# Joining VectorE's and GpSimd's weighted expert sums one step later in the first feed-forward

## What is computed

```
gates        = top-2 of softmax(x @ router_w + router_b), renormalised, zero elsewhere
expert_out_e = gelu(x @ expert_w[e] + expert_b[e])            e = 0..7
combined     = sum over e of gates[:, e] * expert_out_e
x            = layernorm(x + combined @ out_w + out_b)
```

## Time and profile before

| | us |
|---|---|
| median of 3 timed runs | 1030.12 (1030.11 to 1031.32) |
| the profiled execution's own time | 1035.02 |
| its span in the trace | 1033.2 |

### The profile page before, as it was taken

How to read it: one execution, slowest core, us unless ns; L and a number is a source line. 1 busy time by engine, 2 the same in 40 slices (tenths; PEclk the granted TensorE clock), 3 DMA queues, 4 the chain that set the end, 5 groups by cost and what they waited for, 6 DMA issues and landing times.

```text
span 1033.2 us, 23457 instructions
## 1 busy us (share of the span) xinstructions
PE 925.1 (90%) x8745; PEld 626.5 (61%) x8745; DVE 822.4 (80%) x2400; ACT 629.7 (61%) x1560; POOL 373.7 (36%) x605
## 2 busy tenths in 40 slices
PE   6888888887877988998899999999999999999996
PEld 4667676666663444433555566666666666667654
DVE  6999998989986687765799988888888888733566
ACT  6999998989862344343666655555555555432543
POOL 4333342530422545444233333333333333310085
PEclk8999999999986999999999999999999999999999
DMA  7202121100000000000266755555555655510001
GB/s 267 63 23 63 43 63 43 46 20 2 2 2 1 1 1 1 1 1 1 56 125 121 123 100 96 100 97 96 103 103 102 98 97 100 95 36 1 1 32 52
DMA packets 174626, 61.41 MB, mean 59 GB/s; under 512 B 169248, under 2 KB 170800, under 8 KB 174384
## 3 DMA queue, kind: packets, MB, share of 16 engines
q1 hardware_dynamic: 174512, 59.90, 28.7%
HBM read 15.83 MB, written 2.10 MB: 17 GB/s over the span
## 4 chain that ended last, share of the span: by engine, by line
PE 47%; DVE 31%; ACT 6%; POOL 5%; DMA 5%; issue 5%; SPq 0%; POOLq 0%; DVEq 0%; ACTq 0%
PE bank L353 11%; PE bank L355 11%; PE bank L354 11%; DVE s_sb L1135 7%; DMA pt_lo<-w_lo 5%; DVE pt_lo L1092 5%; DVE scr L1122 3%; DVE scr L1092 3%; PE bank L668 3%; PE bank L670 3%; PE bank L669 3%; DVE w_lo L1153 2%; ACT s_sb L850 2%; ACT scr L803 2%; POOL scr L1598 2%
## 5 line engine op out<-in xcount | busy, mean ns | idle before, releaser
L1135 DVE CUSTOM_DVE_ANT_0 s_sb<-bank,consts 128x512 f32<-128x512 f32 (+3 forms) x512 | 227.9, 481 | 23.3 <-PE bank L355 15.0
L852 ACT ACTIVATE s_sb<-s_sb,nm 128x512 f32<-128x512 f32 (+3 forms) x256 | 141.4, 553 | 103.8 <-DVE nm L1135 102.4
L353 PE MATMUL bank<-w_hi,scr 128*128 128x256 bf16 (+1 forms) x576 | 174.2, 302 | 5.1 <-DVE lg_sb L1299 2.6
L355 PE MATMUL bank<-w_hi,scr 128*128 128x256 bf16 (+1 forms) x576 | 173.6, 301 | 0.0
L354 PE MATMUL bank<-w_lo,scr 128*128 128x256 bf16 (+1 forms) x576 | 173.6, 301 | 0.0
L803 ACT ACTIVATE scr<-bank 128x256 bf16<-128x256 f32 (+4 forms) x256 | 120.2, 487 | 76.1 <-PE bank L670 44.5
L850 ACT ACTIVATE s_sb<-s_sb,nm 128x512 f32<-128x512 f32 (+3 forms) x256 | 141.2, 584 | 13.5 <-DVE nm L1135 13.4
L1628 POOL TENSOR_SCALAR wqkv_hi<-s_sb,rr 128x512 bf16<-128x512 f32 (+3 forms) x128 | 65.6, 532 | 141.7 <-DVE rr L1159 141.7
L1092 DVE TENSOR_TENSOR pt_lo<-bank,pt_hi 128x512 bf16<-128x512 f32 (+1 forms) x192 | 108.4, 592 | 7.6 <-ACT pt_hi L803 7.6
L1092 DVE TENSOR_TENSOR scr<-bank,scr 128x256 bf16<-128x256 f32 (+1 forms) x160 | 80.6, 525 | 40.8 <-ACT scr L803 40.4
L403 PE MATMUL bank<-scr 128*128 128x512 bf16 (+3 forms) x256 | 61.7, 306 | 50.9 <-DVE nm L1135 49.4
(11 more groups left out here) (160 smaller groups left out, 2348.6 us busy)
## 6 DMA issues: line engine op xcount, KB each, us to landing
scr<-wall_in SPq DMA_DIRECT2D x19, 512.0 KB, 3.8
x_tok<-x_tok_in SPq DMA_DIRECT2D x1, 2048.0 KB, 9.8
scr<-x_t_in SPq DMA_DIRECT2D x3, 512.0 KB, 9.4
out<-x_tok SPq DMA_DIRECT2D x3, 512.0 KB, 2.6
scr<-wqkv_in SPq DMA_DIRECT2D x2, 384.0 KB, 4.0
pt_hi<-w_hi SPq DMA_TRANSPOSE x32, 3.3
pt_lo<-w_lo SPq DMA_TRANSPOSE x32, 3.4
pt_hi<-wqkv_hi SPq DMA_TRANSPOSE x32, 3.4
```

The costliest lines, as they stand in the source:

```text
L353: pe.matmul(out, l_hi, r_hi, start=start, stop=False, skip_group_check=check)
L355: return pe.matmul(out, l_lo, r_hi, start=False, stop=stop, skip_group_check=check)
L852: last = act.activation(at, at, ACT.Exp, bias=nm[:, j % 2, qt:qt + 1], scale=-1.0, accum_out=rs[:, j % 2, qt:qt + 1])
L1135: last = dve.tensor_tensor_reduce(s_sb[j % 2][:, S_OFF[qt]:S_OFF[qt] + w], bank[turn][:, col:col + w], mask[:, 512 - w:512], -scale, HUGE, ...
```

## The change

`join_halves` moves out of the end of step n on DVE. It now stands in step n+1, behind the x1 low part, `route`, the x2 low part and `mix(n+1, 0)`, and ahead of `joined(n+7, 1)` and of the cm low part, which needs the sum. The join gets a semaphore of its own, `join`, that counts one a tile, and `mul` counts five a tile where it counted six. PE's cm turn waits for `join`, and so does GpSimd before it writes `pc` again. The number of arithmetic instructions is unchanged on every engine.

```diff
-MIX = DVE_X + 1
...
                 elif kind == "cm":
-                    pe.wait_ge(m["mul"], MIX * (t + 1))
+                    pe.wait_ge(m["join"], t + 1)
                     src = comb[t % 2]
...
-                hold(act, m["mul"], MIX * (t - 1) + min(2 * p + 2, DVE_X))
+                hold(act, m["mul"], DVE_X * (t - 1) + min(2 * p + 2, DVE_X))
...
-                        dve.wait_ge(m["mul"], MIX * t + x)
+                        dve.wait_ge(m["mul"], DVE_X * t + x)
...
             def join_halves(t):
                 dve.wait_ge(m["psum"], (NX - DVE_X - 1) * (t + 1))
-                dve.wait_ge(m["mul"], MIX * t + DVE_X)
-                dve.tensor_tensor(comb[t % 2], comb[t % 2], pc[t % 2], ALU.add).then_inc(m["mul"], 1)
+                dve.wait_ge(m["mul"], DVE_X * (t + 1))
+                dve.tensor_tensor(comb[t % 2], comb[t % 2], pc[t % 2], ALU.add).then_inc(m["join"], 1)
...
                 if here:
                     mix(n, 0)
+                if 0 <= behind < NT:
+                    join_halves(behind)
                 if 0 <= ahead < NT:
                     joined(ahead, 1)
...
                 if routed:
                     gate((n + 4) // TT)
-                if here:
-                    join_halves(n)
...
-                    hold(pool, m["mul"], MIX * (t - 1))
+                    hold(pool, m["join"], t - 1)
```

More of the change, by code:

```diff
@@ L268, in build @@
             "rc", "cc", "tp", "thi", "tlo", "o1", "o2", "r1", "r2", "agg1", "agg2", "rstd1", "rstd2", "x1", "x2", "xb",
-            "lg", "lgc", "lgd", "ex", "gates", "f", "ge", "mul", "pmul", "psum", "dve", "pool")}
+            "lg", "lgc", "lgd", "ex", "gates", "f", "ge", "mul", "join", "pmul", "psum", "dve", "pool")}
         e = {n: sem(f"ffn_{n}") for n in (
```

## The result

The changed kernel is slower: 1034.62 us against 1030.86 us (medians of 6 runs each), ratio 1.0033 with a 95% interval of 1.0018 to 1.0048. The forecast was 1029.9 us with a range up to 1033.1; the measured time lies outside it, on the slower side.

The account below looks back on a forecast made before the run. PE was taken to wait 1.07 us per ordinary step behind DVE's join, with DVE the bound in routed steps. Terms 0.3 - 2.5 - 2.2 + 1.3 + 1.0 + 1.9 = -0.2 us gave 1029.9 us, range 1027.0 to 1033.1.

Parts of the forecast that it names:

- What bounds the kernel: DVE idles 32.3 us for GpSimd's last addition before the join; PE feels 1.07 us of an ordinary step.
- Ordinary steps: Steps 2, 5, 6, 9 and 10: PE's cm turn comes earlier, 0.5 us gained each, -2.5 us in all.
- Steps 0 and 1: Step 1 has no x2 turn, so the products come earlier, into GpSimd's additions: +0.3 us.
- Routed steps: Steps 3 and 7: L1299 runs before the join, so first_project follows at once; -1.1 us each, -2.2 together.
- Steps 4 and 8: Behind routed steps: 1.44 us of work stands before the join, 0.65 us given back each, +1.3 for both.
- Steps 11 and 12: Products meet GpSimd's last additions, about +0.7 us, and +0.3 at step 12: +1.0 us.
- Late steps: Steps 13 to 16: the join stands behind the products, 0.45 to 0.5 us lost each, +1.9 us.
- The clock: Slower rival: PE's clock halves behind long waits before cm turns, 1.6 us a fall; two give 1033.1 us; chance 0.2.
- The argument against it: Against the clock rival: over steps 11 and 12 PE idles 2.16 of 14 us and the clock stays full.
- my own step for tiles 3 and 7: In steps 4 and 8, PE now waits about 2 us before the cm turn.
- That the meetings do not happen: Faster rival: DVE's products fall between GpSimd's additions; -3.7 us in all, 1026.4 us; chance 0.25.
- That the wait keeps its old length in its new place: Slower rival: the join holds up `joined` and the cm low part, ordinary steps gain nothing; 1032.4 us; chance 0.05.

Follow-up runs that it names:

- the run without the bias add: Changed kernel with GpSimd's bias add handling 1 of 256 channels: 1025.79 us in one execution, ordinary steps 9.22 us against 9.57.
- The changed kernel with fillers: Changed kernel plus 20 unread matmuls on PE ahead of the cm turns of tiles 3, 7 and 11: 1030.17 us, ratio 0.9985 to the kernel before.
- these comparisons: Changed kernel against the kernel before, timed on two occasions: 1034.62 us, ratio 1.0033 (6 runs each), then 1034.17 us, ratio 1.0026 (12 runs).
- the placement where it pays: Join at its new place only for tiles 1, 2, 4, 5, 6, 8 and 9, otherwise at its old: 1027.16 us, ratio 0.9963 to the kernel before.

## Why the prediction was wrong

*What bounds the kernel.* Right: DVE's 32.3 us of waiting were mostly slack, PE felt about 1 us of an ordinary step, and in late steps there was nothing to win.

*Ordinary steps: mis-sized.* Forecast -0.5 each, measured -0.9 in step 2, -0.8 in steps 5 and 6, -0.7 in 9 (where no fall lies in it), -0.5 in 10. I let both products be lengthened by an instruction of GpSimd; in steps 2, 5, 6 and 10 only the second one is (0.83 us), and GpSimd's sum is earlier than before. The mechanism, that a meeting makes DVE wait, holds and is worth 0.35 us of a step, as the run without the bias add shows.

*Steps 0 and 1* together, forecast +0.3, went from 14.9 us on average to 15.3, with 14.8 to 15.6 in single profiles; at the same clock it is the 0.4 us worked out above. In step 1 both products are lengthened (0.82 and 0.83 us). *Routed steps* gained 1.2 each instead of 1.1. *Steps 4 and 8* gave back 0.45 instead of 0.65 each; the product that took 1.01 us before meets nothing now. *Steps 11 and 12* cost 0.75 and 1.1, 1.85 together instead of 1.0: behind the router of step 11 as well the products stand between the chain's end and the turn, and there the chain ended no earlier (the join came 11.15 us behind the last turn instead of 10.04, which is the 1.1 us of x2 low part and products). *Late steps* cost 0.55, 0.55, 0.55 and 0.37 us, 2.0 in all against 1.9. The fourth came out near by luck: I put it down to the products, and step 16 has none.

With these sizes and no fall of the clock the sum is -1.0 us, against -0.2 forecast. The changed kernel with fillers agrees: from step 2 on its stage is 1.35 us shorter than before, and steps 0 and 1 cost 0.4; the rest of its -1.8 us is the scatter of those two steps. So the position terms were too dark by 0.8 us, and still the kernel came out slower.

*The clock: the step that failed.* The forecast's sum puts the falls of PE's clock behind the new waits at nothing. I had the mechanism as a rival, its place (behind the cm turns of tiles 3, 7 and 11), its price (1.6 us; measured 1.55 to 1.85) and the count from which it decides, two. But I gave it 0.2, and left it out of the forecast. Two falls are what four of five profiles show, one the fifth: nine falls, 3.0 us an execution. With the -1.0 us of the positions this makes the stage's +2.0. The argument against it was the failing one: that PE idled 2.16 of 14 us in steps 11 and 12 at full clock said nothing of waits of 0.7 and 2.7 us within 6 us, since those were of 0.62 and 1.47 us; my own step for tiles 3 and 7 had put the longer ones there ("PE now waits about 2 us before this turn"). A fall was on record behind the 1.90 us wait; a longer wait should have been expected to bring one. Two falls on the forecast's sum give 1033.1 us, which was the end of the range. The first median was 1.5 us above that, the second 1.1. Part of this is the base: the kernel before, 1030.12 us in the forecast, had 1030.86 and 1031.71 us in these comparisons. Against it the change is +3.4 and +2.7 us, where the rival has +3.0. That this fits so well is partly luck, as its positions were 0.8 us too dark and the stage shows +2.0. Of the rest, 0.7 to 1.4 us, the intervals (1.2 to 1.5 us to either side) don't say whether it is more than the scatter of the stages behind.

*A slip.* The forecast's own range, 1028.1 to 1032.1, lies around the 1030.1 of before and not around the forecast of 1029.9; nothing hangs on the 0.2 us.

*The other rivals.* That the meetings do not happen fell with the 0.83 us product. That the wait keeps its old length in its new place fell with the table of waits.

## What to carry to other kernels

Moving a wait behind other work pays only in those rounds of a pipeline in which the work can be done while one waits; in rounds where the awaited data is there first, the work ahead of the wait is simply added to the path. So go through the kinds of steps one by one (first, ordinary, with router, behind the router, last), and place the instruction for each kind; look too at what else stands ahead of the new place in the last step, where the next stage has begun. Before counting on idle time that a change gathers into one long wait of TensorE, look at the granted clock behind the longest waits in the profile: gains of 0.5 to 1.2 us in seven steps, less the losses in the others, came to 1.0 us, and two falls of 1.7 us took more than that.

## What the runs showed of the hardware

- A fall of PE's clock to 1.2 GHz costs 1.55 to 1.85 us of a step when it lies behind a wait of 1.8 to 2.7 us on PE's own chain, and 1.0 us behind the shorter wait of the placement where it pays (11.28 against 10.24 us). In steps 4 and 8 of the kernel before, where it lies in front of a wait for DVE, it costs at most about 0.4 us, as worked out above.
- Whether it comes behind a given wait changes from execution to execution of the same kernel (behind tile 3 in one of five, behind 7 and 11 in four of five). Over all profiles, 13 of 19 cm turns behind a wait of 2.58 to 2.71 us without fillers had a fall.
- Matmuls into columns of PSUM that nobody reads, put into the wait, kept the clock at 2.4 GHz in all nine places where they stood (six in waits of 2.6 to 2.7 us, three in waits of 1.5 to 1.7 us), without delaying the turn behind them by more than 0.01 us.
- An instruction of DVE with two operands in SBUF that meets one of GpSimd ends 0.28 us after it: the join took 0.93 us instead of 0.42, a product 0.83 us instead of 0.48, and 0.48 again when the bias add was cut to one channel.
